# Decoder block on one Trainium2 core: the order of work on GpSimd's queue in the attention loop

## Chip, core and metric

The kernel runs on one core of a Trainium2 chip. The metric is the device time of one execution in microseconds (us). The engines are TensorE (PE in the profile), VectorE (DVE), ScalarE (ACT), GpSimd (POOL) and SyncE (SP), which issues most DMAs. Each engine works through its own queue in order; semaphores tie the queues together.

## What is computed

32 sequences of 256 tokens with 256 channels (float32) pass through three residual layers, each followed by a layer norm. The reference, cut to what matters:

```
# layer 1: a complex decaying recurrence along the sequence axis (32 steps), per token and channel
conv = sum over past n of c**n * x        # c = exp(-exp(lmlg)) * exp(i*theta), plus a start state
x = layernorm(x + conv.real * x)
# layer 2: cross attention, 16 heads of 16 channels, context ctx
Qp, Kp, Vp = relu(x@Wq+bq), relu(ctx@Wk+bk), relu(ctx@Wv+bv)
out = softmax(q k^T / 4) v + Qp
x = layernorm(x + ln_g * (out-mean)/sqrt(var+eps) + ln_b)
# layer 3: each token goes to the nearest of 8 centroids (argmin of a distance), and to that expert
xn  = x * scale * rsqrt(mean(x*x) + 1e-6)
ids = argmin(|xn|^2 + |c|^2 - 2 xn@c.T)
out = (a * silu(g)) @ down_w[ids]  with  a, g = split(xn @ up_w[ids])
x = layernorm(out + x)
```

## The kernel before

There are two phases. Phase 1 is a loop over the 32 sequences (`step(t)`, t from -2 to 34), written out by hand for each engine as a software pipeline: in one step TensorE, VectorE and ScalarE work on the attention scores of sequence t, on the exponentials and sums of t-1, and on what comes before and after of other sequences. Inside a step VectorE, ScalarE and TensorE go through the 16 heads (`h`), with the other work put between heads. Phase 2 (`experts`) goes over 71 tiles of 128 rows, sorted by expert.

In a step, n = t+1, a = t-2 and b = t-3. GpSimd does these parts, in this order:

- `conv_products(t+3)` (L701): the double product of the recurrence, 128x1024, from `state` and `decay` into `by_re`. It, `conv_real`, `conv_imag` 0 and 1 (L709, L717, L720) and `conv_input` (L727, which adds the next x) are the five instructions of one step of the recurrence. None is there from t = 29 on.
- `weigh(b)` (L759): `xw` = row times scale, waits for VectorE's `row`. ScalarE squares `xw` and sums it into `nx` (L951).
- the addition of the bias `b_bc` to `x1` (L789), for `y2` of VectorE.
- `cut(n)` (L777): the low piece of q, `q_lo`, which SyncE stores to DRAM (L572) and reads back, with q's and k's other pieces, as the stacked operands `q_st` and `k_st` of the scores (L585, L586).
- `offset(b)` (L768): `dist` = centroid norms plus `nx`. VectorE's `pick` (L1434 on) starts from it.
- `conv_real`, the root of the first layer norm (L734, L736), `conv_imag` 0, `cut(n+1)` of the keys, `conv_imag` 1.
- the root `rsx` of the norm inside attention, of a (L734, L736). VectorE's `y2` (L1368, two instructions, written to `oq`) waits for it; the moments `mv2` of the second layer norm follow from `y2` in VectorE's order, behind x1, the statistics and two score maxima.
- two indirect DMAs (L809), which scatter the 256 rows of b into the experts' buckets. They wait for VectorE's slots (`slots`, L1471), which need TensorE's ranks.
- `conv_input(t+3)`, the root of the second layer norm of a (`rstd2`: L734, L736), and `rms(a)` (L745 to L751), which writes one more column of `row`.

VectorE writes `row` of a (L1302) at the start of the next step, as that step's b, once `rstd2` is there; then two score maxima (L1287) and `u` (L1310, state plus one, times x). `row` and `slot` have two buffers each, and who writes one waits for the scatter of two sequences earlier. ScalarE takes the exponentials from one set of score banks, VectorE the maxima from the other; TensorE's scores of a head wait for the maximum of two heads before.

In the tail (t from 32 on) VectorE also splits the expert weights (`lower`, L1398, 128x2048 each).

Of the kernel before, what the change touches and what calls it, by code (L numbers as in the profile page):

```python
# [81 lines left out]
def build(nc, x, ctx_in, lmlg, theta, last_conv, Wq, bq, Wk, bk, Wv, bv, ln_g, ln_b, ffn_scale, centroids, up_w, down_w, out):  # L82
    stack = ExitStack()
    with stack:
# [36 lines left out]
        def sb1(name, shape, dt=F32):  # L121
            return phase1.enter_context(nc.sbuf_tensor(name, shape, dt))
# [67 lines left out]
        mv2 = sb1("mv2", [P, NTC, 2])  # L190
        rs2 = sb1("rs2", [P, 2, NTC])
# [38 lines left out]
        def wait(eng, name, item, per=1, j=None):  # L230

            if not item.runtime and item.k >= SEQ:
                item, j = Item(0, SEQ - 1), per
            wait_value(eng, name, item.times(per, per if j is None else j))
# [11 lines left out]
        def wait_ring(eng, sm, item, ring, per):  # L246

            if not item.runtime:
                while item.k >= SEQ:
                    item = item - ring  # L250
            wait_value(eng, sm, item.uses(ring) * per)
# [11 lines left out]
        def active(item):  # L263
            return item.within(0, SEQ)
# [271 lines left out]
        with nc.Block() as block:  # L536
# [121 lines left out]
            def _(pool):  # L658
# [35 lines left out]
                def conv_products(item):  # L694

                    if not active(item):
                        return
                    wait(pool, "conv", item - 1, 5)
                    if item.k == 1:
                        wait(pool, "x1_ok", item - 1, 2)  # L700
                    g.tensor_tensor(by_re[:, :, :, :], state[:, 0].unsqueeze(1).to_broadcast(both), pair_b, ALU.mult).then_inc(s["conv"], 1)  # L701
# [20 lines left out]
                def conv_input(item):  # L722
                    if not active(item):
                        return
                    wait_ring(pool, x_in[item.mod(2)], item, 2, 16)
                    wait(pool, "conv", item, 5, 4)
                    g.tensor_tensor(state[:, 0], state[:, 0], xt[:, item.mod(2)], ALU.add).then_inc(s["conv"], 1)  # L727

                def rstd(item, ready, per, mv, rs, done):

                    if not active(item):
                        return
                    wait(pool, ready, item, per)
                    g.tensor_scalar(rs[:, 0], mv[:, :, 1], LN_EPS, None, ALU.add).then_inc(s[done], 1)  # L734
                    wait(pool, done, item, 2, 1)
                    g.tensor_tensor(rs[:, 1], rs[:, 0], neg_half[:, :].to_broadcast([P, NTC]), ALU.pow).then_inc(s[done], 1)  # L736

                def rms(item):

                    if not active(item):  # L740
                        return
                    p = item.mod(2)
                    wait(pool, "rstd2", item, 2)
                    wait_ring(pool, scat[p], item - 2, 2, 16 * NTC)
                    g.tensor_tensor(ms2[:, 0], mv2[:, :, 1], rs2[:, 1], ALU.mult).then_inc(s["rms"], 1)  # L745
                    wait(pool, "rms", item, 4, 1)
                    g.tensor_tensor(ms2[:, 1], ms2[:, 0], rs2[:, 1], ALU.mult).then_inc(s["rms"], 1)
                    wait(pool, "rms", item, 4, 2)
                    g.tensor_scalar(ms2[:, 2], ms2[:, 1], RMS_EPS, None, ALU.add).then_inc(s["rms"], 1)
                    wait(pool, "rms", item, 4, 3)  # L750
                    g.tensor_tensor(row[:, p, :, C], ms2[:, 2], neg_half[:, :].to_broadcast([P, NTC]), ALU.pow).then_inc(s["rms"], 1)  # L751

                def weigh(item):

                    if not active(item):
                        return
                    wait(pool, "x2_ok", item, 2)
                    wait(pool, "nx_ok", item - 1, 2)
                    g.tensor_tensor(xw[:, :, :], row[:, item.mod(2), :, 0:C], scale_bc[:, :].unsqueeze(1).to_broadcast([P, NTC, C]),  # L759
                                    ALU.mult).then_inc(s["xw_ok"], 1)  # L760

                def offset(item):

                    if not active(item):
                        return
                    wait(pool, "nx_ok", item, 2)
                    wait(pool, "pick", item - 1, PICK, 2)
                    g.tensor_tensor(dist[:, 0], cent_norm[:, :].unsqueeze(1).to_broadcast([P, NTC, E]),  # L768
                                    nx[:, :].unsqueeze(2).to_broadcast([P, NTC, E]), ALU.add).then_inc(s["offset"], 1)
# [9 lines left out]
                def step(t):  # L779
                    n, a, b = t + 1, t - 2, t - 3  # L780
                    first = t.k < 0
                    if first:
                        rstd(t + 2, "ln1", 4, mv1, rs1, "rstd1")
                    conv_products(t + 3)
                    weigh(b)
                    if active(a):
                        wait(pool, "x1_ok", a, 2)
                        wait(pool, "x1T_pe", a)
                        g.tensor_tensor(x1[:, a.mod(4)], x1[:, a.mod(4)], b_bc[:, :].unsqueeze(1).to_broadcast([P, NTC, C]),  # L789
                                        ALU.add).then_inc(s["x1b_ok"], 1)  # L790
                    if n.k > 0:
                        cut(n, q32[:, :, :], q_hi, q_lo, "q_ok", "q_cut", q_out)
                    offset(b)
                    conv_real(t + 3)
                    if not first:
                        rstd(t + 2, "ln1", 4, mv1, rs1, "rstd1")
                    conv_imag(t + 3, 0)
                    if n.k + 1 > 0:
                        cut(n + 1, k32[:, :, :], k_hi, k_lo, "k_ok", "k_cut", k_out)
                    conv_imag(t + 3, 1)  # L800
                    rstd(a, "lnx", 4, mvx, rsx, "rstdx")
                    if active(b):

                        p = b.mod(2)
                        wait(pool, "slot_ok", b, SLOT)
                        wait(pool, "id_ok", b)
                        wait(pool, "rms", b, 4)
                        for c in range(NTC):
                            g.indirect_dma_start(out=buckets[:, :], out_offset=bass.IndirectOffsetOnAxis(ap=slot[:, p, c:c + 1], axis=0),  # L809
                                                 in_=row[:, p, c, :], in_offset=None, bounds_check=PAD - 1,  # L810
                                                 oob_is_err=False).then_inc(scat[p], 16)
                    conv_input(t + 3)
                    rstd(a, "ln2", 4, mv2, rs2, "rstd2")
                    rms(a)

                steps(pool, step)
                gpsimd2(pool)
# [688 lines left out]
```

## Time and profile before

| | |
|---|---|
| median of 3 runs | 1245.58 us (1243.9 to 1256.25) |
| the profiled execution | 1246.19 us, of which the span is 1244.4 us |
| PE busy | 1112.3 us (89%) |
| VectorE busy | 953.2 us (77%) |
| GpSimd busy | 778.6 us (63%) |
| ScalarE busy | 668.7 us (54%) |
| mean granted clock of TensorE | 0.94 |

### The profile page before, as it was taken

The page shows a single profiled execution, that of the slowest core. Times are in us where ns is not written, and L with a number is a line of the kernel's source. Part 1 is how long each engine was busy: PE and PEld are TensorE (multiplying, and loading weights), DVE is VectorE, ACT ScalarE, POOL GpSimd, SP SyncE. Part 2 cuts the span into 40 slices and gives each one's busy share as a digit, 9 for nine tenths or more (in the row PEclk, how much of TensorE's full clock was granted, in tenths as well). Part 3 has the DMA queues.
Part 4 walks back from the last instruction along what each step waited for, and adds up shares of the span by engine and source line. Part 5 has one row for each costly group of instructions (what it writes and reads, how often), then busy time and mean ns, then how long its engine had stood idle before and what let it go on. Part 6 is the DMA issues. An engine that isn't in the chain of part 4 may idle for free.

```text
span 1244.4 us, 27483 instructions
## 1 busy us (share of the span) xinstructions
PE 1112.3 (89%) x8030; PEld 820.1 (66%) x8061; DVE 953.2 (77%) x2416; ACT 668.7 (54%) x1416; POOL 778.6 (63%) x932
## 2 busy tenths in 40 slices
PE   3799999999999999999999998853999999999996
PEld 2566666666666666666666666532888888888885
DVE  7458888999999999999999997863555555555553
ACT  4257766767777777777767766731222222222221
POOL 4645878878978888988978954461333333333333
PEclk9779999999999999999999998656999999999998
DMA  5757667766556556556656554042111111111110
GB/s 131 170 145 206 176 176 192 197 160 163 142 142 154 141 152 163 143 143 162 151 138 159 133 130 109 11 153 60 48 51 48 43 51 51 49 47 49 50 51 19
DMA packets 90825, 144.91 MB, mean 116 GB/s; under 512 B 12662, under 2 KB 78335, under 8 KB 84512
## 3 DMA queue, kind: packets, MB, share of 16 engines
q1 hardware_dynamic: 83616, 126.09, 39.6%
q0 software_dynamic: 6528, 16.99, 4.6%
q8 instruction: 55, 0.90, 0.3%
q10 hardware_dynamic: 576, 0.53, 0.2%
q14 instruction: 50, 0.41, 0.1%
HBM read 91.44 MB, written 53.03 MB: 116 GB/s over the span
## 4 chain that ended last, share of the span: by engine, by line
PE 42%; DVE 33%; issue 9%; POOL 7%; DMA 6%; SPq 2%; ACT 1%; POOLq 0%; DVEq 0%; ACTq 0%
DVE neg_max_sb L1287 12%; PE Y L454 10%; PE G L422 8%; PE A L422 8%; DVE oq L1416 4%; DVE u L1310 3%; DMA neg_max<-nm_row 3%; PE S L1055 3%; POOL buckets L809 3%; PE M L1012 3%; PE GT L432 2%; POOL state L727 2%; PE O L1004 2%; DVE stx L1271 2%; DVE st L1271 1%
## 5 line engine op out<-in xcount | busy, mean ns | idle before, releaser
L1287 DVE TENSOR_REDUCE neg_max_sb<-S 128x2 f32<-128x512 f32 x512 | 327.9, 681 | 52.9 <-PE S L1055 52.1
L888 ACT ACTIVATE probs<-T 128x512 f32<-128x512 f32 x512 | 278.0, 594 | 139.9 <-PE T L1068 124.2
L1055 PE MATMUL S<-k_st,q_st 48*128 48x256 f32 x1024 | 216.1, 320 | 39.3 <-DVE neg_max_sb L1287 34.6
L1055 PEld LDWEIGHTS S<-k_st,q_st 48*128 48x128 f32 x1024 | 147.0, 193 | 117.2 <-issue 78.1
L1068 PE MATMUL T<-q_st,k_st 49*128 49x256 f32 x1024 | 212.1, 320 | 7.4 <-ACT probs L888 3.5
L1068 PEld LDWEIGHTS T<-q_st,k_st 49*128 49x128 f32 x1024 | 146.9, 193 | 23.6 <-ACT probs L888 15.2
L399 ACT ACTIVATE gT<-GT 128x512 f32<-128x512 f32 x71 | 42.5, 598 | 208.2 <-PE GT L432 208.2
L1004 PE MATMUL O<-probs,v_aug 128*32 128x256 f32 x2048 | 145.4, 404 | 0.7 <-ACT probs L888 0.7
L378 POOL DMA_INDIRECT out<-res,token x71 | 76.4, 1076 | 103.3 <-DVE res L499 98.8
L454 PE MATMUL Y<-dn_sb,gT 128*128 x568 | 134.2, 379 | 0.8 <-ACT gT L399 0.8
L809 POOL DMA_INDIRECT buckets<-row,slot x64 | 69.6, 1087 | 85.3 <-DVE slot L1471 75.0
L454 PEld LDWEIGHTS Y<-dn_sb,gT 128*128 128x128 f32 x568 | 107.5, 189 | 18.2 <-issue 1.0
L422 PE MATMUL G<-up_hi,xsT 128*128 x284 | 107.9, 420 | 1.2 <-DVE xsT L504 1.0
L422 PE MATMUL A<-up_hi,xsT 128*128 x284 | 106.2, 415 | 0.0
L383 POOL TENSOR_SCALAR rs<-mv 128x1 f32<-128x1 f32 x71 | 15.9, 224 | 141.2 <-DVE mv L528 141.0
L499 DVE TENSOR_SCALAR res<-y,mv,rs 128x256 f32<-128x256 f32 x71 | 29.4, 413 | 85.8 <-POOL rs L385 85.8
L1004 PEld LDWEIGHTS O<-probs,v_aug 128*32 128x32 f32 x2048 | 55.3, 113 | 52.5 <-ACT probs L888 16.4
L1012 PE MATMUL M<-ctT,wk_sb 128*128 128x256 f32 x256 | 70.0, 421 | 15.3 <-issue 8.7
L701 POOL TENSOR_TENSOR by_re<-state,decay 128x1024 f32<-128x1024 f32 x31 | 73.5, 2371 | 1.2 <-DVE x L1374 0.9
L403 ACT ACTIVATE gate<-G 128x512 f32<-128x512 f32 x71 | 42.4, 597 | 58.9 <-PE G L422 58.9
L1031 PE MATMUL M<-wv_sb,ctT 128*128 128x256 f32 x256 | 71.7, 405 | 2.6 <-issue 0.7
L1012 PE MATMUL M<-x1T,wq_sb 128*128 128x256 f32 x256 | 67.7, 408 | 1.6 <-ACT x1T L903 1.6
(184 smaller groups left out, 2536.4 us busy)
## 6 DMA issues: line engine op xcount, KB each, us to landing
k_st<-k_pieces SPq DMA_DIRECT2D x64, 256.0 KB, 5.0
q_st<-q_pieces SPq DMA_DIRECT2D x64, 256.0 KB, 3.8
xr<-buckets SPq DMA_DIRECT2D x71, 129.0 KB, 2.1
xt<-in_x SPq DMA_DIRECT2D x32, 256.0 KB, 6.1
ct<-in_ctx SPq DMA_DIRECT2D x32, 256.0 KB, 6.4
k_pieces<-k_hi SPq DMA_DIRECT2D x32, 256.0 KB
k_pieces<-k_lo SPq DMA_DIRECT2D x32, 256.0 KB
q_pieces<-q_hi SPq DMA_DIRECT2D x32, 256.0 KB, 2.1
```

The lines of the kernel that those rows point to most:

```text
L378: g.indirect_dma_start(out=out_rows, out_offset=bass.IndirectOffsetOnAxis(ap=token[:, f.mod(2):f.mod(2) + 1], axis=0), in_=res[:, f.mod(2) ...
L422: last = t_.matmul(ps[:, :], xT[:, w, c * P:(c + 1) * P], src[:, bass.ds(off + c * 2 * HID, HID)], start=(k == 0), stop=(k == len(terms) - 1))
L454: last = t_.matmul(Y_ps[:, 0:C], gT[:, m.mod(2), c * P:(c + 1) * P], dn_sb[:, bass.ds(off + c * C, C)], start=(c == 0), stop=(c == HCH - 1))
L701: g.tensor_tensor(by_re[:, :, :, :], state[:, 0].unsqueeze(1).to_broadcast(both), pair_b, ALU.mult).then_inc(s["conv"], 1)
L809: g.indirect_dma_start(out=buckets[:, :], out_offset=bass.IndirectOffsetOnAxis(ap=slot[:, p, c:c + 1], axis=0), in_=row[:, p, c, :], in_of ...
L888: a_.activation(probs[:, h % 8].rearrange("p k t -> p (k t)"), T_ps[h % 2][:, :], ACT.Exp, scale=DH ** -0.5).then_inc(s["exp_ok"], 1)
L1004: last = t_.matmul(O_ps[32 * j:32 * j + 32, (grp % 2) * TOK:(grp % 2 + 1) * TOK], v_aug[:, item.mod(4), kc, h * VW:h * VW + 32], probs[:, ...
L1012: last = t_.matmul(dst[:, oc * TOK:(oc + 1) * TOK], w[:, ic, oc * P:(oc + 1) * P], xT[:, ic, :], start=(ic == 0), stop=(ic == NCH - 1))
L1031: last = t_.matmul(M_ps[1][:, c * C:(c + 1) * C], ctT[:, ic, c * P:(c + 1) * P], wv_sb[:, ic, :], start=False, stop=(c == NTC - 1 and ic = ...
L1055: last = t_.matmul(S_ps[h % 2][:, c * TOK:(c + 1) * TOK], q_st[base:base + STACK, h, c * P:(c + 1) * P], k_st[base:base + STACK, h, :], st ...
L1068: last = t_.matmul(T_ps[h % 2][:, c * TOK:(c + 1) * TOK], k_st[base:base + AUG, h, c * P:(c + 1) * P], q_st[base:base + AUG, h, :], start= ...
L1287: v.tensor_reduce(neg_max[:, cur.mod(2), :, h], S_ps[h % 2][:, :].rearrange("p (c t) -> p c t", c=NTC), AX.X, ALU.max, negate=True).then_i ...
```

## The change

Three things change on GpSimd's queue inside `step`, and nothing else. The scatter's waits and its two indirect DMAs go behind `conv_input`, `rstd2` and `rms`, to the end of the step. The offset goes ahead of q's low piece. From t = 0 on, the double product goes behind `weigh` and the bias; for t below 0 it stays where it was. The order is then: weigh, bias, double product, offset, q's piece, conv_real, first root, conv_imag 0, k's piece, conv_imag 1, lnx root, conv_input, ln2 root, RMS, scatter.

```diff
@@ step(t) of gpsimd @@
-                    conv_products(t + 3)
+                    if first:
+                        conv_products(t + 3)
                     weigh(b)
                     if active(a):
                         wait(pool, "x1_ok", a, 2)
                         wait(pool, "x1T_pe", a)
                         g.tensor_tensor(x1[:, a.mod(4)], x1[:, a.mod(4)], b_bc[:, :].unsqueeze(1).to_broadcast([P, NTC, C]),
                                         ALU.add).then_inc(s["x1b_ok"], 1)
+                    if not first:
+                        conv_products(t + 3)
+                    offset(b)
                     if n.k > 0:
                         cut(n, q32[:, :, :], q_hi, q_lo, "q_ok", "q_cut", q_out)
-                    offset(b)
                     conv_real(t + 3)
...
                     conv_imag(t + 3, 1)
                     rstd(a, "lnx", 4, mvx, rsx, "rstdx")
+                    conv_input(t + 3)
+                    rstd(a, "ln2", 4, mv2, rs2, "rstd2")
+                    rms(a)
                     if active(b):
...
                             g.indirect_dma_start(out=buckets[:, :], out_offset=bass.IndirectOffsetOnAxis(ap=slot[:, p, c:c + 1], axis=0),
                                                  in_=row[:, p, c, :], in_offset=None, bounds_check=PAD - 1,
                                                  oob_is_err=False).then_inc(scat[p], 16)
-                    conv_input(t + 3)
-                    rstd(a, "ln2", 4, mv2, rs2, "rstd2")
-                    rms(a)
```

## Rows read from the trace of the kernel before

**Rows 1.** Stretches: start:end length, busy us and instructions by engine, clock, DMA share, GB/s
```profile
135.17:722.80 587.63, 543.84 (x4833) 374.69 (x4854) 552.92 (x1400) 418.68 (x926) 502.72 (x551) 0.99 0.62 157
722.80:846.28 123.48, 92.30 (x710) 63.09 (x709) 96.62 (x256) 75.86 (x141) 66.79 (x82) 0.71 0.34 93
```
**Rows 2.** Single steps, scatter to scatter: busy PE, PEld, DVE, ACT, POOL, clock, DMA
```profile
512.99:535.76 22.77, 21.11 (x195) 14.73 (x194) 21.77 (x56) 16.64 (x37) 20.27 (x22) 1.00 0.61 152
...
628.19:651.94 23.75, 21.68 (x195) 14.83 (x194) 22.74 (x56) 16.83 (x38) 19.59 (x23) 1.00 0.59 147
...
722.80:745.25 22.45, 21.24 (x195) 14.77 (x194) 20.89 (x56) 16.68 (x38) 13.03 (x18) 1.00 0.53 131
```
**Rows 3.** Waits, whole span: who for whom, us in total, times, longest
```profile
POOL buckets L809 <- DVE slot L1471: 75.0, 31, 3.6
...
DVE row L1302 <- POOL rs L736: 21.8, 28, 2.0
```
**Rows 4.** Timeline of POOL, one step: start, us, instruction, idle before it
```profile
519.30 2.38 POOL L701 TENSOR_TENSOR by_re<-state,decay 128x1024 f32<-128x1024 f32 x1
521.62 1.65 POOL L759 TENSOR_TENSOR xw<-row,scale_bc 128x512 f32<-128x512 f32 x1
...
525.70 0.20 POOL L768 TENSOR_TENSOR dist<-cent_norm,nx 128x16 f32<-128x16 f32 x1
...
533.20 0.96 POOL L736 TENSOR_TENSOR rsx<-rsx,neg_half 128x2 f32<-128x2 f32 x1
535.76 1.08 POOL L809 DMA_INDIRECT buckets<-row,slot  x1 [1.60 <-DVE slot L1471]
537.14 0.98 POOL L809 DMA_INDIRECT buckets<-row,slot  x1 [0.30 <-issue]
538.14 1.30 POOL L727 TENSOR_TENSOR state<-state,xt 128x512 f32<-128x512 f32 x1
539.39 0.24 POOL L734 TENSOR_SCALAR rs<-mv 128x2 f32<-128x2 f32 x1
```
**Rows 5.** Timeline of VectorE, the same step
```profile
519.70 2.52 DVE L1310 SCALAR_TENSOR_TENSOR u<-state,xt 128x512 f32<-128x512 f32 x1
...
526.03 0.36 DVE L1434 SCALAR_TENSOR_TENSOR dist<-M,row,dist 128x8 f32<-128x8 f32 x2
...
534.86 0.88 DVE L1368 SCALAR_TENSOR_TENSOR oq<-o,rsx,x 128x256 f32<-128x256 f32 x2
...
538.34 0.23 DVE L1277 BATCH_NORM_AGGREGATE mv<-st 128x2 f32<-128x6 f32 x2
```
**Rows 6.** Line of `u`: count, duration ns min/median/max, first and last start
```profile
L1310 DVE SCALAR_TENSOR_TENSOR u<-state,xt x32: 681/2512/2544, 13.9 to 729.5; 128x512 f32<-128x512 f32 x32
```
**Rows 7.** Timeline of POOL in the tail
```profile
748.15 0.22 POOL L734 TENSOR_SCALAR rs<-mv 128x2 f32<-128x2 f32 x1 [0.55 <-DVE mv L1277]
...
751.00 1.19 POOL L759 TENSOR_TENSOR xw<-row,scale_bc 128x512 f32<-128x512 f32 x1
...
814.74 2.46 POOL L809 DMA_INDIRECT buckets<-row,slot  x1 [0.30 <-issue]
...
829.18 1.34 POOL L809 DMA_INDIRECT buckets<-row,slot  x1 [0.53 <-issue]
```
**Rows 8.** Timeline of VectorE in the tail
```profile
747.83 0.24 DVE L1277 BATCH_NORM_AGGREGATE mv<-st 128x2 f32<-128x6 f32 x2
...
814.08 2.27 DVE L1398 TENSOR_TENSOR up_sb<-up_sb,up_hi 128x2048 fp32r<-128x2048 f32 x1
```
**Rows 9.** Timeline of POOL in the first step with attention output
```profile
108.98 1.27 POOL L727 TENSOR_TENSOR state<-state,xt 128x512 f32<-128x512 f32 x1
```
**Rows 10.** Timeline of VectorE in that step
```profile
109.01 1.93 DVE L1423 SCALAR_TENSOR_TENSOR o<-oq,mvx,g_bc 128x256 f32<-128x256 f32 x2
```
**Rows 11.** Line of `xs` in the expert stage: count, duration ns min/median/max
```profile
L514 DVE SCALAR_TENSOR_TENSOR xs<-xr,scale_bc x71: 474/477/483, 858.4 to 1219.2; 128x256 f32<-128x256 f32 x71
```
**Rows 12.** Waits of SyncE's DMA queue, from 110 to 850 us
```profile
SPq L241 <- PE T L1068: 79.6, 44, 3.0
```

## The prediction, made before the changed kernel ran

> **What bounds the kernel now.** I cut the trace first into stretches. Of the 1244.4 us span, 587.6 us are 25 equal steps of the attention loop, from the scatter at 135.17 to the one at 722.80, at a granted clock of 0.99; the edit touches only this loop and the 123 us of its tail [rows 1]. One step is 23.5 us on average (587.6 / 25). Cut by step, there are steps of 22.8 and of 23.8 us at a granted clock of 1.00, and the first step in which GpSimd (POOL) has no recurrence work left still takes 22.45 us: with VectorE as it is, TensorE and VectorE together allow hardly less [rows 2].
>
> Next I read who waits for whom. POOL waits for VectorE's slots ahead of the scatter, 31 times, and VectorE waits for POOL's second root ahead of `row`, 28 times, 0.7 us in a usual step [rows 3]. So the two engines stand in one ring: slots, scatter, conv_input, root, row, and VectorE's work up to the next slots. The timelines give its times. POOL runs without a gap from the double product at 519.30 to the end of the lnx root at 534.16, that is 14.86 us, idles 1.60, scatters for 2.36 (535.76 to 538.12), adds the input and takes the root [rows 4]. VectorE has its ln2 moments ready at 538.57, but the root starts at 539.39 only: it stands behind the scatter and conv_input [rows 4, 5]. That is the wait which the edit takes away.
>
> A second thing shows in the durations. `u`, with two inputs in SBUF, takes 0.68 us at the least and 2.51 in the middle [rows 6]: it starts at 519.70, while the double product runs until 521.68, and ends 0.54 after it [rows 4, 5]. VectorE's instruction is held until POOL's is over; then `weigh` is held in turn and takes 1.65.
>
> **The change, part by part.** All of it is order on POOL's queue: no instruction, DMA or semaphore is added or removed. I follow one new step from the end of the ln2 moments (time 0).
>
> 1. *Root and RMS.* POOL has finished conv_input long before and waits for the moments. The tail shows this case: moments done at 748.07, root from 748.15, and `weigh`, the next instruction behind the RMS, from 751.00. So 2.93 us [rows 7, 8].
> 2. *Scatter.* Slots are long ready. Where a scatter follows a root with its slots ready, 0.53 us pass before it starts (829.18). Then 2.36, as now. Together 2.89, so POOL is free at 5.82. The two indirect DMAs land later in the step; their buffers are used again two steps on, so nothing waits for them.
> 3. *Weigh, bias, product, offset, q's piece, and on to the lnx root.* The same instructions, 14.86 us [rows 4]. The product no longer lies on `u`, which now falls on the scatter, so `weigh` is not held: less 0.45 (1.65 against the 1.19 of the `weigh` at 751.00) [rows 4, 7]. That leaves 14.4, and the root ends at 20.22. I keep the other holds inside these 14.86 as they are, since VectorE's order against POOL's is nearly the same there; bounds are 0 and about 1.4 us less.
> 4. *Conv_input* now follows the lnx root at once, 1.30 us, where the scatter's wait stood.
> 5. *VectorE's part.* `y2` waits for the lnx root; from its start to the end of the moments are 3.71 us (534.86 to 538.57) [rows 5].
>
> What it costs besides: the offset now stands behind the product. Before, it ended at 525.90 and VectorE reached `dist` at 526.03, with 0.1 us to spare [rows 4, 5]. New, the offset ends 10.9 us after the moments (5.82, then 1.19 for `weigh`, 1.3 for the bias, 2.4 for the product, 0.2). VectorE is at `dist` 10.2 us after the moments now (526.03 against 538.57 less one step of 22.77); with the 0.7 us wait gone and `u` shorter by up to 1.8 that is 7.7 to 9.5. So it waits 1.4 us or more there: what `u` and `row` gain is given back before it reaches anybody. Below that comes the lnx root: VectorE needs 8.8 us from `dist` to `y2` (526.03 to 534.86) and so arrives at 19.8, before 20.22. POOL sets the step.
>
> The ring is therefore: root and RMS, scatter, POOL's chain, `y2` to the moments. 2.93 + 2.89 + 14.4 + 3.71 = 23.93 us, already more than the 23.5 of now. In place of the wait for slots, POOL waits for moments that exist 3.7 us after the lnx root; conv_input fills 1.3 of it.
>
> **And conv_input is in the way.** When the lnx root ends, POOL's next instruction starts at once and `y2`, also two inputs in SBUF, is released 0.04 us later. The trace of now has just this order once, in the first step with attention output, which scatters nothing: conv_input ran from 108.98 directly behind the lnx root, and the two gain instructions that VectorE started at 109.01 took 1.93 us together instead of the 0.88 of the `y2` pair, which is of the same kind and size [rows 5, 9, 10]. They ended 0.7 us after conv_input had. So `y2` is held until conv_input is over: 1.30 - 0.04 = +1.25 us, and all of it is on the ring. Bounds are 0 (`y2` gets there first) and 1.3. I take 1.25, by the row with the same order. The step becomes 25.2 us.
>
> The Trainium skill (SBUF — State Buffer, the section on the engine ports) says that whichever of the two engines starts first keeps the shared ports for its whole instruction. By it the 0.04 us decide. It would make the scatter hold `u` too, and the trace does not bear that out: `xs`, also with two inputs in SBUF, starts 0.3 us into each output scatter of the expert stage and takes 0.477 us in all 71 cases, 0.483 at most [rows 11].
>
> **SyncE's queue.** q's low piece is ready about 12.1 us after the moments, now 9.9; its store, q's loads and the later ones move by 2.2 us, while the step grows by 1.7. SyncE waits 44 times for TensorE's T before the second halves [rows 12], so the delay is used up there: nothing. If that slack were not there, it would be 0.5 us a step.
>
> **Tail.** Without recurrence work the product and conv_input are gone; root and row come 0.7 to 2 us earlier in five steps, `weigh` and the offset up to 2 later. Nothing, within 5 us.
>
> **Sum.** 25 x (25.2 - 23.5) = +42 us on the profiled execution, which took 1246.2 us (span 1244.4); the median of the runs is 0.6 below it. 1288 us.
>
> **Rivals.** A change under 1% (12 us) can't be told from none.
> - *A, y2 first.* All as above, but `y2` starts before conv_input. Step 24.0, +12 us, 1258 us. For it: both wait for the same instruction, and which engine won such a race differs from step to step (the 22.8 and 23.8 us steps are of this kind). Against it: [rows 9, 10].
> - *B, the holds go away (faster).* The place is POOL's chain of 14.4 us. If `y2` is first and VectorE's two-input instructions fall between POOL's rather than on them, up to 1.4 us of it go. It decides from 0.5 us on, where the ring passes under 23.5; then VectorE's gains of 0.7 (`row`) and 1.8 (`u`) count, down to the 22.45 of [rows 2]. 25 x 1.05 = -26 us, 1220 us. Against it: it needs both at once.
> - *C, the scatter is held by u.* `u` in flight when the scatter starts. In the tail one scatter took 2.46 us instead of 0.98, ending 0.85 after a long two-input instruction of VectorE [rows 7, 8]. Here it would be at most the 0.6 us that `u` lasts: +15 on the main case, 1303 us. The scatter starts at 3.5 (2.93 + 0.53). `u` comes behind four score maxima of 0.64, `row` and `ids` (0.9), so at 3.5 or later: near, but TensorE's scores hold the second pair of maxima back a little, and `u` more likely falls inside the scatter, as `xs` does [rows 11]. The Trainium skill (SBUF — State Buffer, the box on the trap of DMAs issued from GpSimd) says that a VectorE instruction that keeps the shared ports stops GpSimd from writing descriptors. The tail's row agrees.
> - *D, it is a wash.* `y2` first and half of B's holds gone, or slow-clock steps (TensorE-bound) hiding most: 1240 to 1255 us.
>
> **Chances.** Main case 0.55, A 0.17, B 0.10, C 0.08, D 0.10. Slower by over 1%: main, C and over half of A, 0.73; the same: D and most of the rest of A, 0.17; faster 0.10. The range takes in main, A and C with POOL's holds up to 0.6 us a step either way: 1252 to 1306.
>
> **What would show it.** In the steps after: POOL idle before the ln2 root, 2 to 2.5 us a step, and none before the scatter; `u` at 0.7 us; VectorE waiting for `dist` of POOL and for `rsx`; `y2` at 2.1 us for two instead of 0.88, with conv_input beside it; steps of 25 us. Wrong, if `y2` stays at 0.88 (then A), if the offset comes before VectorE is there, or if steps are under 23.5 us.

## The result, and the profile after

The change makes the kernel 9.9% slower: ratio 1.0991, 95% interval [1.0927, 1.1054]. The medians are 1375.53 us after (4 runs, 1367.27 to 1398.28) and 1248.98 us before (4 runs beside them). The profiled execution is the slowest of the four, 1398.28 us at a span of 1396.5, and the ratio leaves it out; the other three took 1367 to 1380, so the trace of the kernel after is of an execution 1 to 2% longer than those.

**The loop took it.** I cut both traces from RMS to RMS. The 25 equal steps (140.50 to 868.12) take 727.6 us, where before they took 587.6 [rows 1]: 140 of the 152 us that the two spans differ by. Of the rest 8.5 us lie in the five steps of the tail (115.9 against 107.4) and 3 in the experts.

Stretches of the kernel after, and two single steps. Columns as in [rows 1, 2]: length, busy PE, PEld, DVE, ACT, POOL with their instructions, granted clock, DMA share, GB/s.
```profile
140.50:868.12 727.62, 629.81 (x4827) 422.57 (x4851) 645.90 (x1401) 427.20 (x926) 481.71 (x551) 0.85 0.50 126
868.12:984.01 115.89, 90.19 (x674) 58.06 (x673) 85.12 (x226) 69.70 (x129) 53.09 (x71) 0.69 0.33 92
...
501.83:531.73 29.90, 25.86 (x200) 17.08 (x201) 25.84 (x58) 17.20 (x38) 19.12 (x23) 0.84 0.47 117
...
561.62:588.06 26.44, 23.48 (x198) 15.94 (x199) 23.52 (x58) 16.96 (x38) 19.45 (x22) 0.87 0.50 127
```
There are two kinds of step. Seven take 26.4 to 26.5 us, eighteen take 29.3 to 30.9 (30.1 on average). Against the 23.5 of before, 25 times 2.95 are 74 us, and the excess of the eighteen over 26.45 is 18 x 3.7 = 66. Both kinds need a cause. The granted clock fell from 0.99 to 0.85 in this stretch.

Waits of the kernel after, whole span: us in total, times, longest.
```profile
POOL rs L734 <- DVE mv L1280: 193.4, 33, 8.0
...
DVE neg_max_sb L1290 <- PE S L1058: 109.9, 79, 8.4
...
DVE dist L1437 <- POOL dist L768: 17.7, 11, 5.1
```
The scatter's wait for slots and `row`'s wait for the root [rows 3] are gone, as meant. In their place GpSimd waits 193 us for VectorE's moments: from its offset on, GpSimd is not what sets the step.

**A short step.** GpSimd's timeline, then VectorE's. In brackets the idle time ahead, and what ended it.
```profile
560.53 0.22 POOL L734 TENSOR_SCALAR rs<-mv 128x2 f32<-128x2 f32 x1 [5.91 <-DVE mv L1280]
...
563.39 1.09 POOL L815 DMA_INDIRECT buckets<-row,slot  x1 [0.17 <-issue]
564.78 1.08 POOL L815 DMA_INDIRECT buckets<-row,slot  x1 [0.30 <-issue]
565.89 1.20 POOL L759 TENSOR_TENSOR xw<-row,scale_bc 128x512 f32<-128x512 f32 x1
...
570.60 0.21 POOL L768 TENSOR_TENSOR dist<-cent_norm,nx 128x16 f32<-128x16 f32 x1
...
572.02 1.26 POOL L709 TENSOR_TENSOR state<-by_re,state 128x512 f32<-128x512 f32 x1
...
575.96 1.67 POOL L777 TENSOR_TENSOR k_lo<-k,k_hi 128x512 fp32r<-128x512 f32 x1
...
579.13 0.71 POOL L736 TENSOR_TENSOR rsx<-rsx,neg_half 128x2 f32<-128x2 f32 x1
579.80 1.27 POOL L727 TENSOR_TENSOR state<-state,xt 128x512 f32<-128x512 f32 x1
```
```profile
564.33 0.68 DVE L1313 SCALAR_TENSOR_TENSOR u<-state,xt 128x512 f32<-128x512 f32 x1
...
570.94 0.36 DVE L1437 SCALAR_TENSOR_TENSOR dist<-M,row,dist 128x8 f32<-128x8 f32 x2 [0.72 <-POOL dist L768]
571.84 1.48 DVE L1444 TENSOR_TENSOR cand<-dist,least 128x16 f32<-128x16 f32 x1
...
575.13 1.37 DVE L1419 TENSOR_TENSOR oq<-o,qn 128x256 f32<-128x256 f32 x1
576.42 1.24 DVE L1454 TENSOR_TENSOR onehot_bf<-expert_no,choice 128x16 bf16<-128x16 f32 x1
579.90 1.45 DVE L1426 SCALAR_TENSOR_TENSOR o<-oq,mvx,g_bc 128x256 f32<-128x256 f32 x1
...
583.17 0.87 DVE L1371 SCALAR_TENSOR_TENSOR oq<-o,rsx,x 128x256 f32<-128x256 f32 x2
...
586.65 0.24 DVE L1280 BATCH_NORM_AGGREGATE mv<-st 128x2 f32<-128x6 f32 x2
```
GpSimd does what was predicted: its lnx root ends at 579.84, 19.4 us after the moments (560.44). But `y2` starts only at 583.17, 3.3 us later and not held. VectorE comes late: from `dist` to `y2` it needs 12.2 us, where before it needed 8.8 [rows 5]. In between stand four instructions with two inputs in SBUF, each held until a large GpSimd instruction is over: `cand` (0.22 unheld) until the real part ends, the second `oq` (unheld 0.61), `onehot` (unheld 0.17) until k's piece ends, and the first of the two gains (unheld 0.47) until conv_input ends. `cand` begins 0.18 us ahead of the real part, still inside q's piece (570.78 to 572.06), and is shut out by both. That is 4.1 us of held time, against 0.7 in the step of [rows 5], where only that `oq` is held much (1.14). The difference, 3.4 us, is what `dist` to `y2` grew by. VectorE waits 0.72 us for the offset, 10.5 us after the moments, and is hardly idle from there to the next moments: the ring is 10.5 (offset) + 12.2 + 3.7 = 26.4. The `oq` of that step, in the kernel before:
```profile
529.06 1.14 DVE L1416 TENSOR_TENSOR oq<-o,qn 128x256 f32<-128x256 f32 x1
```

**A long step.** VectorE, GpSimd, TensorE of the kernel after from 504.9 us on.
```profile
504.90 1.29 DVE L1290 TENSOR_REDUCE neg_max_sb<-S 128x2 f32<-128x512 f32 x2 [2.25 <-PE S L1058]
506.11 5.19 DVE L1313 SCALAR_TENSOR_TENSOR u<-state,xt 128x512 f32<-128x512 f32 x1
```
```profile
505.00 0.97 POOL L815 DMA_INDIRECT buckets<-row,slot  x1 [0.30 <-issue]
506.00 1.19 POOL L759 TENSOR_TENSOR xw<-row,scale_bc 128x512 f32<-128x512 f32 x1
507.14 1.28 POOL L790 TENSOR_TENSOR x<-x,b_bc 128x512 f32<-128x512 f32 x1
508.39 2.36 POOL L701 TENSOR_TENSOR by_re<-state,decay 128x1024 f32<-128x1024 f32 x1
...
519.41 1.27 POOL L777 TENSOR_TENSOR k_lo<-k,k_hi 128x512 fp32r<-128x512 f32 x1 [3.19 <-ACT k L938]
```
```profile
511.96 0.58 PE L1058 MATMUL S<-k_st,q_st 48*128 48x256 f32 x1 [1.72 <-DVE neg_max_sb L1290]
...
513.97 3.75 PE L1015 MATMUL M<-ctT,wk_sb 128*128 128x256 f32 x8 [0.62 <-issue]
```
TensorE's scores come late (2.25), so `u` no longer starts inside the scatter but just after it. There it is held behind weigh, bias and product together, 5.19 us, and ends 0.55 after the product. TensorE idles 1.72 behind it, and then the k projection takes 3.75 us, twice the 1.97 to 1.99 of steps at full clock. GpSimd in its turn idles 3.19 us ahead of k's piece, which needs that projection: such waits come to 45.0 us in 21 over the span, before to 6.8 in 5. The next scores are late again.
```profile
L1313 DVE SCALAR_TENSOR_TENSOR u<-state,xt x32: 681/4629/5881, 14.1 to 873.0; 128x512 f32<-128x512 f32 x32
```
That is the line of `u` of the kernel after (min/median/max), which answers to [rows 6]: 0.68 in the seven short steps, 4.6 to 5.9 in the eighteen long ones.

### The profile page after: what moved, and what is told of

It reads as the page before. It is cut to its first block, busy times and chain, and to the rows that moved or that the text cites. A ratio compares the mean times of both kernels' runs of the same rounds, so it can differ in the third digit from the quotient of the medians.

```text
span 1396.5 us, 27483 instructions
## 1 busy us (share of the span) xinstructions
PE 1202.8 (86%) x8030; PEld 867.7 (62%) x8061; DVE 1049.6 (75%) x2416; ACT 678.1 (49%) x1416; POOL 753.6 (54%) x932
## 4 chain that ended last, share of the span: by engine, by line
PE 46%; DVE 33%; issue 11%; POOL 4%; DMA 3%; SPq 1%; ACT 1%; POOLq 0%; DVEq 0%; ACTq 0%
DVE neg_max_sb L1290 11%; PE Y L454 9%; PE G L422 7%; PE A L422 7%; PE S L1058 5%; PE M L1015 5%; PE O L1007 4%; DVE oq L1419 3%; DVE u L1313 3%; DVE o L1426 3%; PE GT L432 2%; DVE oq L1371 2%; DVE st L1274 2%; PE M L987 2%; DVE x L1377 2%
## 5 line engine op out<-in xcount | busy, mean ns | idle before, releaser
L1058 PE MATMUL S<-k_st,q_st 48*128 48x256 f32 x1024 | 242.8, 348 | 80.4 <-DVE neg_max_sb L1290 72.7
L1058 PEld LDWEIGHTS S<-k_st,q_st 48*128 48x128 f32 x1024 | 165.0, 214 | 179.2 <-issue 92.3
L1071 PE MATMUL T<-q_st,k_st 49*128 49x256 f32 x1024 | 240.5, 348 | 9.9 <-ACT probs L891 8.7
L1071 PEld LDWEIGHTS T<-q_st,k_st 49*128 49x128 f32 x1024 | 165.5, 215 | 23.0 <-ACT probs L891 13.6
L1007 PE MATMUL O<-probs,v_aug 128*32 128x256 f32 x2048 | 163.9, 445 | 0.7 <-ACT probs L891 0.7
L734 POOL TENSOR_SCALAR rs<-mv 128x2 f32<-128x2 f32 x64 | 19.3, 302 | 205.0 <-DVE mv L1280 193.4
L1015 PE MATMUL M<-ctT,wk_sb 128*128 128x256 f32 x256 | 95.2, 537 | 20.4 <-issue 13.8
L1313 DVE SCALAR_TENSOR_TENSOR u<-state,xt 128x512 f32<-128x512 f32 x32 | 106.3, 3323 | 0.0
L1015 PEld LDWEIGHTS M<-ctT,wk_sb 128*128 128x128 f32 x256 | 66.5, 273 | 39.2 <-issue 18.0
L1034 PE MATMUL M<-wv_sb,ctT 128*128 128x256 f32 x256 | 81.6, 450 | 3.8 <-issue 2.3
```

The source lines that it names most:

```text
L1007: last = t_.matmul(O_ps[32 * j:32 * j + 32, (grp % 2) * TOK:(grp % 2 + 1) * TOK], v_aug[:, item.mod(4), kc, h * VW:h * VW + 32], probs[:, ...
L1015: last = t_.matmul(dst[:, oc * TOK:(oc + 1) * TOK], w[:, ic, oc * P:(oc + 1) * P], xT[:, ic, :], start=(ic == 0), stop=(ic == NCH - 1))
L1034: last = t_.matmul(M_ps[1][:, c * C:(c + 1) * C], ctT[:, ic, c * P:(c + 1) * P], wv_sb[:, ic, :], start=False, stop=(c == NTC - 1 and ic = ...
L1058: last = t_.matmul(S_ps[h % 2][:, c * TOK:(c + 1) * TOK], q_st[base:base + STACK, h, c * P:(c + 1) * P], k_st[base:base + STACK, h, :], st ...
L1071: last = t_.matmul(T_ps[h % 2][:, c * TOK:(c + 1) * TOK], k_st[base:base + AUG, h, c * P:(c + 1) * P], q_st[base:base + AUG, h, :], start= ...
L1313: v.scalar_tensor_tensor(u[:, :, :], state[:, 0], 1.0, xt[:, nn.mod(2)], ALU.add, ALU.mult).then_inc(s["u_ok"], 1)
```

## The experiments

Beside the change's three parts they vary one wait or place each. An expectation's own words say what its letters mean. Diffs against the kernel before unless said; times are medians.

**1. The scatter alone, behind the RMS.**
```diff
 rstd(a, "lnx", ...)
+conv_input(t + 3); rstd(a, "ln2", ...); rms(a)
 (scatter of b)
-conv_input(t + 3); rstd(a, "ln2", ...); rms(a)
```

> The kernel before with the scatter alone behind RMS; product and offset where they were. Theory H (holds): an instruction of VectorE with two inputs in SBUF that finds GpSimd busy is kept until GpSimd's queue has a gap, so behind a whole run of instructions. Then u, which starts near the scatter, is short in some steps and in others kept behind product, weigh and bias (some 5 us), and conv_input keeps the gain instructions: steps of 26 to 31 us, 1340 to 1400 us. Theory R (ring only): VectorE is kept by at most one instruction, and only the path moments, RMS, scatter, offset, dist counts. It is 1.25 us longer than in the changed kernel (q's piece lies ahead of the offset), so 28 us a step at full clock and about 1410 us. Forecast of the record (A, y2 first): 1258.

Measured: 1419.39 us (1406 and 1433), longer than with all three parts. That is above theory H's range and near R's 1410, but R's number is met by luck: no step takes 28 us and `u` is kept by more than one instruction. H's mechanism is what the trace shows, with steps up to 32.3 us. One step of it, GpSimd, then the line of `u`:
```profile
426.18 0.97 POOL L812 DMA_INDIRECT buckets<-row,slot  x1 [0.30 <-issue]
427.18 2.37 POOL L701 TENSOR_TENSOR by_re<-state,decay 128x1024 f32<-128x1024 f32 x1
...
431.88 1.25 POOL L777 TENSOR_TENSOR q_lo<-q,q_hi 128x512 fp32r<-128x512 f32 x1
433.11 0.65 POOL L768 TENSOR_TENSOR dist<-cent_norm,nx 128x16 f32<-128x16 f32 x1
```
```profile
L1310 DVE SCALAR_TENSOR_TENSOR u<-state,xt x32: 681/6565/7045, 13.9 to 909.5; 128x512 f32<-128x512 f32 x32
```
The run behind the scatter holds four large instructions here, and `u` is held for all of them: started at 427.26, it took 6.43 us. Its few short steps take 26.43 to 26.45 us, like those of the whole change, though `cand` is not held in them. So the scatter's move by itself costs more than the whole loss, and the two others give a part back behind it.

**2. The product alone, behind weigh and bias.**
```diff
-conv_products(t + 3)
 weigh(b); (bias)
+conv_products(t + 3)
 cut(n, q32, ...)
 offset(b)
```

> The kernel before with the product alone behind weigh and bias; the scatter stays ahead of conv_input. Theory H: u starts 0.4 us after the RMS, now inside weigh, and is kept behind weigh, bias and product: 5 us instead of 2.5 in every step, so +2 to +2.5 us a step, 1295 to 1310 us, more if TensorE's clock falls in the gap. Theory R: u waits for weigh only (1.3 us instead of 2.5), xw is 2.4 us earlier, the offset is where it was: 1235 to 1247 us.

Measured: 1252.84 us, ratio 1.0101 [1.0048, 1.0154]: 6 us above R's range, far below H's. `u` is held by weigh alone: median 1.33 us, at most 2.69 (once, behind the product). That a run always holds `u` to its end is refuted. Steps are 22.7 or 23.7 to 24.0; `onehot` is held more often (0.79 us on average from 160 to 700 us, 0.51 before).

**3. The scatter back,** against the kernel after; product and offset stay where the change put them.
```diff
-conv_input(t + 3); rstd(a, "ln2", ...); rms(a)
 (scatter of b)
+conv_input(t + 3); rstd(a, "ln2", ...); rms(a)
```

> The kernel after with one of its three moves undone: the scatter stands between the lnx root and conv_input again, and product and offset stay where the change put them. Theory (the move of the scatter is what costs; with a wait for slots ahead of the scatter, VectorE's instructions reach their places as before, and the other two moves are worth the 1% that the product alone cost): 1243 to 1262 us, steps of 22.7 to 24, u held by one instruction, at most 2.7 us. Rival (the moves work on one another: product ahead of the offset makes dist late in either order): 1275 to 1310 us.

Measured: 1274.63 us, ratio 1.0211 [1.0162, 1.026]. That is at the rival's end. Of the 10% the scatter's place makes 8; the two other parts together cost 2, not 1. `u` is 1.34 us in the median. Now GpSimd has the same three instructions in the same order as after, with the RMS ahead of them instead of the scatter:
```profile
512.24 0.71 POOL L751 TENSOR_TENSOR row<-ms,neg_half 128x2 f32<-128x2 f32 x1
512.91 1.19 POOL L759 TENSOR_TENSOR xw<-row,scale_bc 128x512 f32<-128x512 f32 x1
514.07 1.73 POOL L790 TENSOR_TENSOR x<-x,b_bc 128x512 f32<-128x512 f32 x1
515.75 2.38 POOL L701 TENSOR_TENSOR by_re<-state,decay 128x1024 f32<-128x1024 f32 x1
```
`u` starts at 513.31, 0.40 behind weigh's start, and takes 1.34; then the bias is held in its turn (1.73 instead of 1.28). After, a `u` that started as late as 0.67 us behind weigh's start still took 4.63, and the bias 1.27. So the long hold needs the scatter ahead.

**4. The offset alone, ahead of q's piece.**
```diff
+offset(b)
 cut(n, q32, ...)
-offset(b)
```

> The kernel before with the third part alone: the offset ahead of q's piece. Theory (VectorE had its offset 0.1 us in time before, and GpSimd has 1.6 to 2.4 us of idle time ahead of the scatter to lose): no change, 1238 to 1256 us. Rival (the offset now waits for ScalarE's sum of squares and q's piece moves onto VectorE's cand or oq, which are held by it): cand or oq 0.4 us longer or more, 1256 to 1275 us.

Measured: 1268.95 us, ratio 1.0177 [1.0127, 1.0227]. The theory of no change falls and the rival's time holds; its mechanism holds in part. With q's piece behind the offset, what stands behind q's piece comes later against VectorE: `cand` is held by the real part (at 462.35 us for 0.80, until 0.03 after it), `onehot` by k's piece.
```profile
L1451 DVE TENSOR_TENSOR onehot_bf<-expert_no,choice x32: 159/1248/1281, 125.8 to 863.1; 128x16 bf16<-128x16 f32 x32
L1441 DVE TENSOR_TENSOR cand<-dist,least x32: 165/802/1220, 121.8 to 862.5; 128x16 f32<-128x16 f32 x32
```
Before, their medians were 0.18 and 0.22 us. Steps of 24.2 to 24.4 become the rule.

**5. `u` first.** Against the kernel after:
```diff
+if not first: wait(pool, "u_ok", t + 2)
 weigh(b)
```

> The changed kernel, with one wait more: GpSimd waits for u of the next sequence but one ahead of weigh. Theory H: u takes 0.7 us in every step, the steps of 30 us go, and all are as the short ones (26.45 us) or up to 0.6 above: 1300 to 1325 us. Theory R: u was no cause; the wait holds weigh and the offset back by up to 1 us a step: 1380 to 1400 us.

Measured: 1342.06 us, ratio 1.0802 [1.0649, 1.0955]. `u` takes 0.68 to 0.69 in every step. Steps are 26.4 and 27 to 28.2 us; those of 29 to 31 are gone. The time is above the theory's 1325, which had no steps of 28 us in it.

**6. A pause in the run.** Against the kernel after, GpSimd waits for its own weigh:
```diff
 weigh(b)
+if not first and active(b): wait(pool, "xw_ok", b)
 (bias)
```

> The kernel after, in which GpSimd waits between weigh and bias for its own semaphore of xw (that is, until weigh has ended). Nothing else differs. Theory Q (VectorE's two-input instruction is shut out as long as GpSimd's instructions follow one another without a gap, so a pause in that run lets it in): a u that starts late in the scatter is held by weigh alone, 1.3 to 2.5 us instead of the 4.6 to 5.9 of the kernel after; TensorE no longer idles 1.7 us behind it, the steps of 29 to 31 us go, 26.4 to 27.5 stay: 1310 to 1345 us. Rival (what shuts VectorE out is the scatter before the run, however the run is made up): u 4.6 us and more in half of the steps, as after, and 1365 to 1385 us.

Measured: 1340.44 us, ratio 1.0743 [1.0667, 1.082]; the theory's range. One step of it, GpSimd:
```profile
419.24 0.97 POOL L817 DMA_INDIRECT buckets<-row,slot  x1 [0.30 <-issue]
420.23 1.19 POOL L759 TENSOR_TENSOR xw<-row,scale_bc 128x512 f32<-128x512 f32 x1
421.50 1.62 POOL L792 TENSOR_TENSOR x<-x,b_bc 128x512 f32<-128x512 f32 x1
```
`u` starts at 419.92, inside the second indirect DMA, and takes 2.06 us where it took 5.6 after; the bias is then held in turn. Without the wait the bias starts 0.05 us before weigh has ended (507.14 against 507.19), with it 0.08 after, and `u` is let in behind weigh.

**7. TensorE's phase.** Against the kernel after, on TensorE; GpSimd's queue is as after.
```diff
 if h == 1: ...
-    if active(a): weighted_sum(a, 3)
+if h == 2 and active(a): weighted_sum(a, 3)
```

> The kernel after, in which TensorE does the last quarter of the weighted sum of the step before behind the scores of heads 2 and 3 instead of ahead of them (1.07 us at full clock, 1.9 at half). Nothing of GpSimd's queue differs. Theory P (the phase: the long steps come from scores that arrive after the first scatter has ended, and feed themselves through the idle TensorE): u starts inside the first scatter and takes 0.68 us, the long steps of 29 to 31 us go, steps of 26.4 stay: 1315 to 1340 us. Rival (where u falls is not what TensorE's order sets, or the clock is low for another reason): u is held as after, 1360 to 1390 us. If the ring through weigh, product and offset sets the short steps, neither goes under 26 us a step.

Measured: 1340.75 us, ratio 1.0746 [1.0677, 1.0814]. The time is just above the theory's 1340. `u` is 0.68 in all 25 steps, so where the scores fall decides the hold. Three ways to the same, 1340 to 1342: the holds of `u` cost some 30 us against the 1367 to 1380 of after. Steps of this kernel:
```profile
491.84:518.14 26.30, 23.62 (x195) 15.96 (x194) 23.37 (x58) 16.62 (x38) 19.32 (x22) 0.87 0.50 127
518.14:544.44 26.30, 21.78 (x198) 14.68 (x196) 23.37 (x58) 17.32 (x39) 19.32 (x22) 1.00 0.61 143
...
597.72:625.96 28.24, 24.50 (x201) 16.06 (x199) 23.34 (x58) 17.63 (x39) 19.78 (x22) 0.91 0.51 124
```
26.30 us at 0.87 and at 1.00: the short step is not TensorE's. In the long one TensorE begins at half clock (the q projection takes 2.54 us), VectorE waits 3.74 for scores and the offset 1.47 for ScalarE: that is left over without any hold of `u`. That it is the clock's price is read from this step; no run varies the clock alone.

**8. The gains first.** Against the kernel after:
```diff
 rstd(a, "lnx", ...)
+if active(a): wait(pool, "y_ok", a, 4, 2)
 conv_input(t + 3)
```

> The changed kernel, with one wait more: GpSimd waits for VectorE's two gain instructions ahead of conv_input. Theory H: the first gain instruction falls from 1.45 to 0.48 us, y2 and the moments come 1.0 us earlier in every step, GpSimd loses nothing (it idles 5.9 us behind conv_input): 25 to 26 us less, about 1345 us. Rival: the gain instruction waits for something else (lnx moments) or the time is given back at the next hold: no change, 1370 us.

Measured: 1313.39 us, ratio 1.0571 [1.0425, 1.0717]. The gains take 0.48 us, most steps 25.4 to 26.1. That is 32 us under the theory's 1345, since most of the long steps go too. One hold of 0.98 out of the ring takes 1.1 off the short step, and `u` is held behind the run (5.2 to 6.0 us) in 3 steps only.

**9. Three waits,** against the kernel after:
```diff
+wait(pool, "u_ok", t + 2)
 weigh(b)
...
+wait(pool, "pick", b, PICK)
 cut(n + 1, k32, ...)
...
+wait(pool, "y_ok", a, 4, 2)
 conv_input(t + 3)
```

> The kernel after with GpSimd waiting three times: for u ahead of weigh, for onehot ahead of k's piece, for the gains ahead of conv_input. Theory R (with the holds gone from u, onehot and the gain, VectorE needs some 10 us from dist to y2 instead of 12.2, and the ring by way of GpSimd that the prediction reckoned, 24 to 24.5 us, sets the step): steps 24.1 to 24.7, GpSimd's idle time ahead of the ln2 root 2.5 to 4 us, 1283 to 1303 us. Rival (the holds are moved to cand and oq, or TensorE's clock sets the step): steps of 25.4 and more, 1308 us and more, as with the wait for the gains alone.

Measured: 1299.24 us, ratio 1.042 [1.0359, 1.0481]. In the range, but the steps are 25.0, not 24.1 to 24.7: `dist` to `y2` is 10.8 us (658.43 to 669.22), with `cand` and the second `oq` still held. GpSimd idles 3.75 ahead of the root, and VectorE waits 0.70 for the offset, as in the kernel after.

**10, 11. A fourth wait,** for `cand`'s first instruction, and in the second kernel for both (5 instead of 4):
```diff
+wait(pool, "pick", b, PICK, 4)
 conv_real(t + 3)
```

> The kernel with three waits (for u, onehot and the gains), and a fourth: GpSimd waits for VectorE's cand ahead of the recurrence's real part, so that cand (1.19 us in the middle stretch there, 0.22 in the kernel before) can't be held. Theory R (VectorE's holds from dist to y2 are all of what lengthens the ring over the prediction's): cand 0.2 us, dist to y2 about 9.6 us instead of 10.8, steps 23.9 to 24.4 instead of 25.0, near the prediction's 24.0 without conv_input's hold; 1270 to 1285 us. Rival (held time is only moved on, to oq behind cand, or TensorE sets the 25.0): steps 24.9 to 25.3, 1295 to 1305 us.

> The kernel with four waits, the fourth now for both instructions of cand instead of the first. With the first alone, the hold of 1.1 us went from cand's first to its second instruction, and the step stayed at 25.0. GpSimd's real part starts about 0.6 us later than there. Theory M (some two-input instruction of VectorE pays in each unbroken run of GpSimd's; the next is the second oq, already held by 0.9): VectorE gains 1.1 us at cand and loses part of it behind the later run; dist to y2 9.6 to 10.3 us, steps 24.3 to 24.7 in the calm stretches, where GpSimd's lnx root, now 0.6 later, comes to set the end; 1285 to 1303 us. Rival (the hold is handed on once more, to oq's first or the maximum behind it, or TensorE sets 25.0): steps 25.0 or more, 1303 to 1315 us.

Measured: 1308.59 us, ratio 1.0513 [1.045, 1.0575], and 1305.29 us, 1.0477 [1.0385, 1.057]. Neither gains; the short steps are 25.0 and 24.9, as with three waits (most of the second's take 25.4 to 25.7), and both theories fall. Taking the hold from one instruction need not shorten the ring. VectorE with the first, then with the second:
```profile
663.39 0.25 DVE L1452 TENSOR_TENSOR cand<-dist,least 128x16 f32<-128x16 f32 x1
...
664.11 1.25 DVE L1456 SCALAR_TENSOR_TENSOR cand<-cand,expert_no 128x16 f32<-128x16 f32 x1
...
666.56 1.51 DVE L1427 TENSOR_TENSOR oq<-o,qn 128x256 f32<-128x256 f32 x1
```
```profile
614.29 0.16 DVE L1456 SCALAR_TENSOR_TENSOR cand<-cand,expert_no 128x16 f32<-128x16 f32 x1
...
615.65 0.65 DVE L1427 TENSOR_TENSOR oq<-o,qn 128x256 f32<-128x256 f32 x1
...
618.67 1.38 DVE L1434 SCALAR_TENSOR_TENSOR o<-oq,mvx,g_bc 128x256 f32<-128x256 f32 x1
...
620.04 1.17 DVE L1475 TENSOR_TENSOR place<-place,onehot_bf 128x16 f32<-128x16 f32 x1
```
The hold is handed on: from `cand` to its second instruction, and when both and the `oq` are free, to the gain and `place`. `dist` to `y2` stays at 10.8 us with the first and 10.6 to 10.7 with the second. GpSimd's run from the offset to conv_input is nearly unbroken, and VectorE has eight such instructions to bring past it.

**12. The same account in the kernel before.** Its steps of 23.8 us hold `onehot` behind k's piece, those of 22.8 don't. Five kernels: the kernel before with a wait for `onehot` alone; with the product moved as in 2 as well; the order "weigh first" without and with that wait; and this with the wait for `cand` of 10.
```diff
+wait(pool, "pick", b, PICK)
 cut(n + 1, k32, ...)
```
```diff
-conv_products(t + 3)
 weigh(b)
-(bias)
+conv_products(t + 3)
 cut(n, q32, ...)
 offset(b)
+(bias)
```

> The kernel before with one wait added: GpSimd waits for VectorE's onehot ahead of the cut of k's low piece. In the kernel before, steps of 23.8 us hold onehot for 1.26 us and steps of 22.8 don't. Theory (that hold is what makes the step long): onehot 0.17 to 0.18 in every step, nearly all steps 22.8, 1220 to 1236 us. Rival (GpSimd's later k piece falls on another instruction of VectorE, the second oq or the gains, and holds that instead; in the kernel with weigh first the wait took 1 us off a step and left it at 23.2): 1243 us and more.

> The kernel before with the product behind weigh and bias, and GpSimd waiting for onehot ahead of k's piece. Theory (the product's move alone costs 1% because it brings onehot into k's piece in more steps, 0.79 us against 0.51 in the middle stretch): with that hold gone, and u at 1.3 us, at or under the kernel before with the onehot wait: 1228 to 1242 us. Rival (the product's move costs through the offset, which comes later): 1245 to 1256 us.

> The kernel before with its scatter where it was, and on GpSimd weigh ahead of the double product, q's piece and the offset ahead of the bias. What is told apart is whether the hold of u has a length that the order behind the RMS sets. Theory Q: u, which starts at the first instruction behind the RMS, is held by weigh alone, 1.3 us instead of 2.5, and dist has its offset in time; steps between 22.5 and 23.5, 1222 to 1240 us. Rival (as in the kernel with the product alone moved: the product behind weigh is held and delayed as much as u gains, or the 23.8 us steps come from onehot's hold behind k's piece, which stays): 1243 to 1255 us.

> The same order as b1_weigh_first, and GpSimd waits for VectorE's onehot ahead of the cut of k's low piece, so that k's piece can't hold onehot (1.26 us in the steps of 23.8, 0.18 in those of 22.8). Theory: onehot is 0.18 us in every step, the steps of 23.8 us go and nearly all take 22.5 to 22.9: 1213 to 1232 us. Rival (what POOL loses by the wait comes back through k's piece and rsx): at or above b1_weigh_first's time, 1240 to 1260 us.

> The kernel b2_onehot_first (weigh, product, q's piece, offset, bias; wait for onehot) with a wait of GpSimd for cand ahead of the recurrence's real part. Theory (the 23.2 us steps there are VectorE's, cand being held 1 us in each): cand 0.2 us, steps 22.45 to 22.8, 1225 to 1242 us. Rival (the second oq or TensorE sets them): 1247 to 1260 us.

| kernel | us | ratio to before [95%] | `cand`, `onehot` median |
|---|---|---|---|
| before + wait | 1241.49 | 0.9945 [0.9918, 0.9972] | 0.22, 0.17 |
| product moved + wait | 1242.03 | 0.9994 [0.9958, 1.0031] | 0.22, 0.17 |
| weigh first | 1269.53 | 1.019 [1.0141, 1.0239] | 1.21, 1.25 |
| weigh first + wait | 1254.12 | 1.0044 [1.001, 1.0079] | 1.21, 0.16 |
| the same + wait for `cand` | 1267.49 | 1.0177 [1.013, 1.0224] | 0.17, 0.17 |

The wait for `onehot` takes 15 us off the weigh-first order and 0.5% off the kernel before, whose steps at full clock are all 22.8 to 23.1 with it. That is clear of noise and small, and 5 us above the 1236 expected at most: steps at clock 0.93 remain at 23.8 to 24.0. "Product moved + wait" is just at the end of its theory's range: with `onehot` free in both, the product's move costs about half a per cent (0.9994 against 0.9945, intervals that just overlap), where it cost one in 2. The three weigh-first kernels all missed their theories, the first and the last also their rivals' ranges, upward. Weigh first shortens `u` from 2.5 to 1.3 us and loses by `cand`, 24.1 us a step. The wait for `cand` again only moved the hold, to the gains (0.72 us on average instead of 0.53), and cost 13 us.

## Why the prediction was wrong

The direction was right and the size was not: 1288 us was predicted, 1252 to 1306 the range, and it took 1375.5.

- *The failed step: "VectorE needs 8.8 us from `dist` to `y2` (526.03 to 534.86) and so arrives at 19.8, before 20.22. POOL sets the step."* The arrival was `dist`'s new time plus an old duration. That duration has holds in it, and which instructions are held depends on where GpSimd stands, which the change moves by microseconds. It was 12.2 us. So POOL's chain up to the lnx root did not set the step; POOL's part up to the offset and VectorE's from there did, 26.4 us against the forecast 25.2: 30 us of the miss. That held time is the cause is shown by the gains' wait (8) and the three waits (9), which took 1.1 and 1.4 us off the short step. That all of the 12.2 could be brought back is refuted by 10 and 11.
- *"`u` now falls on the scatter", 0.7 us.* True in 7 steps of 25. In 18 it came just behind the first indirect DMA and cost 4.6 to 5.9. Rival C asked whether `u` would hold the scatter; it did not ask what a `u` that missed it would meet. (C's own case occurs in experiment 7: at 167.93 us the second indirect DMA found `u` in flight and took 1.33 us instead of 0.97, ending 0.85 behind `u`, as in the tail's row.) Experiments 5 to 7, in which no `u` was held to a run's end, gave some 30 us back.
- *TensorE's clock stood in no term.* The sum took 0.99 in the loop as given. It went to 0.85, and the rest of the distance, some 20 us, is what experiment 7 still shows with `u` at 0.68: its 25 steps took 676.2 us, where 25 of 26.30 are 657.5. How much clock a longer step costs, and how much of these 20 us is the clock's, was not measured by itself.
- *"The offset: it waits 1.4 us or more"*: 0.7 us at 10.5 (10.9 predicted). Of each of the two smaller moves the prediction thought only of what waits for it. Alone they cost 1.0% and 1.8%, both by holds.
- *`y2` held by conv_input, +1.25.* The size was near (0.98), the victim wrong: it held the first gain, and `y2` took 0.87. [rows 9, 10] showed conv_input against gains, and should have been read as that. Rival A (`y2` unheld) was right on this point, and its 1258 us wrong by the first point.
- *Right:* root and RMS in 2.9 us; scatter without a wait (gap 0.17 instead of 0.53); the lnx root 19.4 us after the moments (20.2 predicted, 14.0 of chain instead of 14.4); 3.7 from `y2` to the moments; both old waits gone. GpSimd's idle time ahead of the root was 5.91, not 2 to 2.5, which is the first point seen from the other side.
- *Tail and experts, "within 5"*: 8.5 and 3 us more.

The Trainium skill (SBUF — State Buffer, the section on the engine ports) says that whoever starts first keeps the shared ports for its whole instruction. The trace agrees where VectorE waits for one instruction (`onehot`, the gain, and `u` in 2 and 3). Behind a scatter it does not: GpSimd kept VectorE out over three and four instructions, 4.6 to 7.0 us, also where `u` had begun up to 0.7 us ahead of the first of them. Nor does it for `cand` in the short steps, which began 0.18 us ahead of the real part and was held by it.

## What to carry to other kernels

When a queue is reordered on one of two engines that hold each other's instructions, a duration read across several instructions of the other engine is not a constant: take it apart into unheld times, and place each two-input instruction against the new order. Look for the place where a miss feeds itself (late scores, `u` behind the run, idle TensorE, half clock, late scores): here 18 steps of 25 were of the long kind. A wait that makes the run pause can be worth more than the gap it opens, but only for an instruction with nothing held behind it: otherwise the hold is handed on.

## What the runs showed of the hardware

- `u`, when it started later than about 0.3 us into GpSimd's second indirect DMA, or in the first instruction behind it, and GpSimd paused nowhere, waited until the whole back-to-back run was over: 4.63 to 5.95 us with three large instructions, 5.83 to 7.04 with four. One step, in the tail of experiment 1, differs: `u` was let in behind two of three (3.25 us at 909.48), and q's piece was held in its turn (1.73). Started in the first indirect DMA, or within 0.15 us of the start of the second, it took 0.67 to 0.72; so did every `u` of experiment 5, where GpSimd waited behind the DMAs. Behind the RMS the same run held it for one instruction, 1.34 us. A wait between weigh and bias, with a gap of 0.08 us in the run, ended the hold behind weigh. Why the scatter makes the difference stays open.
- The other way round, the second indirect DMA, when it started with `u` in flight, took 1.16 to 1.36 us instead of 0.97 and ended 0.84 to 0.85 behind `u` (six cases in experiments 5, 6 and 7).
- Whether a small instruction is held turns on a few hundredths of a microsecond: `cand` beginning 0.17 to 0.19 us ahead of the real part was held (1.47 to 1.49 us) in all seven short steps of the kernel after; beginning 0.15 ahead of it in experiment 5 (417.90) it was not (0.23), nor once in experiment 9 at 0.17 (434.42).
- TensorE idle for 1.7 us behind such a hold was followed by work at half clock (a projection 3.75 us instead of 1.99).
